# c turned by VectorE in 32x32 blocks and the convolution evicted by ScalarE, in a two-layer kernel on one core

## What is computed

```python
# layer 0: a channel mixing drawn from cond, then a feed-forward with a top-1 of 4 low-rank experts
agg_w = einsum('bk,koi->boi', softmax(mlp(cond)), weight)
y     = einsum('boi,bih->boh', agg_w, x) + agg_b[:, :, None]
x     = x + y @ W_up.T + one_hot(argmax(y @ gate.T + ebias)) . (y @ A) @ B
# layer 1: a grouped convolution along the positions (9 taps, 4 groups of 8 channels), then top-2 of 8 experts
c     = conv1d(x, wconv, pad=4, groups=4) + (cond @ c_weight.T)[:, :, None] + fside[None, :, None]
x     = x + c @ W_base.T + b_base + sum over the two best experts of p_e * (c @ A_e) @ B_e
```

## Time and profile before

| what | value |
|---|---|
| median of 3 runs | 400.89 us (400.55 to 401.44) |
| the profiled execution's own time | 400.67 us |
| its span in the trace | 398.9 us |
| granted TensorE clock, mean | 0.996 |
| PE, weight loads, DVE, ACT, POOL busy | 96%, 89%, 68%, 26%, 40% |
| DMA | 77 GB/s, queue 1 26.1% of 16 engines |

### The profile page before, as it was taken

The page is one execution under the profiler, slowest core; times in us unless marked ns, Lnnn a source line. Parts: engine busy times, 40 slices in busy tenths (PEclk is TensorE's granted clock), DMA queues, the critical chain, the costliest instruction groups (busy, mean ns, idle before and its releaser), DMA issues.

```text
span 398.9 us, 8234 instructions
## 1 busy us (share of the span) xinstructions
PE 383.5 (96%) x2615; PEld 354.9 (89%) x2615; DVE 270.0 (68%) x837; ACT 103.5 (26%) x251; POOL 160.4 (40%) x146
## 2 busy tenths in 40 slices
PE   4999999999999999999999999999999999999995
PEld 2887999989999999999999999999999999999984
DVE  4568667657766676777667767676677676766553
ACT  4733222222122222221222222212222222222211
POOL 4314444243444443334444433344444333444420
PEclk9989999999999999999999999999999999999999
DMA  5803342212122222112222321222222212222111
GB/s 131 268 15 114 116 140 81 80 32 65 64 78 79 79 79 74 37 61 65 79 79 79 79 78 30 63 66 79 79 79 79 58 50 64 66 79 79 54 53 55
DMA packets 31404, 30.75 MB, mean 77 GB/s; under 512 B 4740, under 2 KB 21556, under 8 KB 31392
## 3 DMA queue, kind: packets, MB, share of 16 engines
q1 hardware_dynamic: 31184, 30.19, 26.1%
q0 software_dynamic: 208, 0.41, 0.4%
HBM read 13.79 MB, written 8.40 MB: 56 GB/s over the span
## 4 chain that ended last, share of the span: by engine, by line
PE 86%; issue 2%; DVE 1%; DMA 1%; ACT 1%; SPq 0%; DVEq 0%
PE ps_base L912 18%; PE ps_conv L865 17%; PE ps_up L829 15%; PE ps_base L917 9%; PE ps_up L834 7%; PE ps_mix L789 7%; PE ps_base L883 5%; PE ps_ct L894 4%; PE ps_up L776 2%; PE ps_turn L768 2%; DMA xq<-x1p 1%; PE ps_turn L760 1%; SPq L293 0%; DVE x1p L598 0%; DVE c L680 0%
## 5 line engine op out<-in xcount | busy, mean ns | idle before, releaser
L364 POOL TENSOR_TENSOR y_lo<-y,y_hi 128x512 fp32r<-128x512 f32 x31 | 40.1, 1293 | 198.8 <-ACT y_hi L407 198.8
L912 PE MATMUL ps_base<-base_hi,c_hi 128*128 128x392 f32 (+1 forms) x256 | 77.7, 320 | 1.1 <-ACT c_hi L458 1.1
L912 PE MATMUL ps_base<-base_lo,c_hi 128*128 128x392 f32 (+1 forms) x256 | 75.0, 310 | 0.0
L829 PE MATMUL ps_up<-up_hi,y_hi 128*128 128x292 f32 (+1 forms) x256 | 67.9, 292 | 0.7 <-ACT y_hi L407 0.7
L829 PE MATMUL ps_up<-up_lo,y_hi 128*128 128x292 f32 (+1 forms) x256 | 67.5, 291 | 0.0
L508 DVE TENSOR_TENSOR mix_w<-gsum,quad 128x64 f32<-128x64 f32 x64 | 48.1, 753 | 6.6 <-DVE gl L648 5.3
L371 POOL TENSOR_TENSOR x1b<-x1p,bbase_s 128x512 f32<-128x512 f32 x32 | 50.1, 1566 | 4.1 <-DVE ot L688 4.1
L912 PEld LDWEIGHTS ps_base<-base_hi,c_hi 128*128 128x128 f32 x256 | 48.4, 189 | 1.5 <-DVE ot L688 1.5
L829 PEld LDWEIGHTS ps_up<-up_hi,y_hi 128*128 128x128 f32 x256 | 48.9, 191 | 0.9 <-ACT y_hi L407 0.9
L829 PEld LDWEIGHTS ps_up<-up_lo,y_hi 128*128 128x128 f32 x256 | 48.9, 191 | 0.0
L917 PE MATMUL ps_base<-base_hi,c_lo 128*128 128x392 f32 (+1 forms) x256 | 48.4, 311 | 0.0
(11 more groups left out here) (156 smaller groups left out, 626.7 us busy)
## 6 DMA issues: line engine op xcount, KB each, us to landing
xt<-in_x SPq DMA_DIRECT2D x32, 256.0 KB, 3.0
xq<-x1p SPq DMA_DIRECT2D x128, 64.0 KB, 2.2
out_x<-ot SPq DMA_DIRECT2D x32, 256.0 KB, 3.0
rows<-agg_rows SPq DMA_DIRECT2D x2, 597.0 KB, 4.1
wup_raw<-in_L_ffn_W_up SPq DMA_DIRECT2D x2, 512.0 KB, 5.5
wbase_raw<-in_L_ffn_W_base SPq DMA_DIRECT2D x2, 512.0 KB, 5.2
rows<-agg_rows SPq DMA_DIRECT2D x1, 598.0 KB, 4.7
rows<-agg_rows SPq DMA_DIRECT2D x1, 256.0 KB, 4.0
```

Of the source, the lines that this page charges most:

```text
L364: pool.tensor_tensor(y_lo[:], y32[:], y_hi[:], ALU.subtract).then_inc(ylo_done, 1)
L829: pe.matmul(into, y_hi[:, k], w[:, k, cols], start=(k == 0 and w is up_hi), stop=False, skip_group_check=True)
L912: pe.matmul(ps_base[:, j, 0:width], c_hi[:, q], w[:, q, j, 0:width], start=(q == 0 and w is base_hi), stop=False, skip_group_check=True)
```

## The change

- `c32` is written by ACT, `conv_out`: four activations (Identity, with `biasT` as bias from SBUF), one a batch, each 128x128 from `ps_conv`.
- `c32` is turned by DVE, `turn_c`: two transposes of 128x256, which turn each 32x32 block by itself and write `ps_ct`. The four transposes of PE are gone, and its other stages keep their order.
- `ps_ct` then holds on partitions (q, m modulo 32) and in columns (batch, m divided by 32, o): the chunks of the base product are blocks of 128 neighbouring positions and no longer remainders. So POOL reorders `wbase_raw`, `a1_raw` and `g1_raw` in the setup (`base_p` in four copies of 128x512, two of them ahead of the first `y_lo`; `a1_p`; `g1_p`), and the fill of the layer 1 gate moves from the place before the first step to the end of the fills.
- `ot` is summed in two halves of 128x256 (`out_sum`), and each bank of `ps_base` is freed by its own half.

```diff
+            pool.wait_ge(in_base[0], 16)
+            for dc in range(KC // 2):
+                pool.tensor_copy(by_chunk(base_p[:, dc]), chunk_rows(wbase_raw[:, dc])).then_inc(basep_ready, 1)
             pool.wait_ge(y32_done, 1)
             pool.wait_ge(yhi_done, 1)
             pool.tensor_tensor(y_lo[:], y32[:], y_hi[:], ALU.subtract).then_inc(ylo_done, 1)
+            pool.wait_ge(in_base[1], 16)
+            for dc in range(KC // 2, KC):
+                pool.tensor_copy(by_chunk(base_p[:, dc]), chunk_rows(wbase_raw[:, dc])).then_inc(basep_ready, 1)
+            pool.wait_ge(in_a1, 16)
+            pool.tensor_copy(by_chunk(a1_p[:]), chunk_rows(a1_raw[:])).then_inc(a1p_ready, 1)
+            pool.wait_ge(in_gate, 16)
+            pool.tensor_copy(by_chunk(g1_p[:]), chunk_rows(g1_raw[:])).then_inc(g1p_ready, 1)
...
+            def conv_out(t):
+                act.wait_ge(conv_done, t + 1)
+                after(act, ct_done, t * 2)
+                for b in range(SPT):
+                    act.activation(c32[:, b], ps_conv[:, 0, b * NM:(b + 1) * NM], ACT.Identity,
+                                   bias=biasT[:, bass.ds(t * SPT + b, 1)]).then_inc(c32_done, 1)
...
+            def turn_c(t):
+                after(dve, clo_done, t)
+                for half in range(2):
+                    dve.wait_ge(c32_done, t * SPT + (half + 1) * (SPT // 2))
+                    dve.transpose(ps_ct[:, 0, half * HALF:(half + 1) * HALF],
+                                  c32[:, half * (SPT // 2):(half + 1) * (SPT // 2)].rearrange("p b m -> p (b m)"))\
+                        .then_inc(ct_done, 1)
...
                 if once(i - 1):
-                    dve.wait_ge(conv_done, i)
-                    after(dve, ct_done, i - 1)
-                    for half in range(2):
-                        b2 = slice(half * SPT // 2, (half + 1) * SPT // 2)
-                        dve.tensor_tensor(c32[:, b2], ps_conv[:, 0].rearrange("p (b m) -> p b m", b=SPT)[:, b2],
-                                          biasT[:, bass.ds((i - 1) * SPT + half * (SPT // 2), SPT // 2)].unsqueeze(2)
-                                          .to_broadcast([P, SPT // 2, NM]), ALU.add).then_inc(c32_done, 1)
+                    turn_c(i - 1)
                 if once(i - 2):
-                    dve.tensor_tensor(ot[:, par].rearrange("p (j d) -> p j d", j=2), ps_base[:, :, 0:HALF],
-                                      x1b[:, par].rearrange("p (j d) -> p j d", j=2), ALU.add)\
-                        .then_inc(out_done, 1)
+                    out_sum(i, par, 0)
+                    out_sum(i, par, 1)
...
-                if once(i - 1):
-                    after(pe, clo_done, i - 1)
-                    for b in range(SPT):
-                        if b % (SPT // 2) == 0:
-                            pe.wait_ge(c32_done, (i - 1) * 2 + 1 + b // (SPT // 2))
-                        mm = pe.transpose(ps_ct[:, 0, b * P:(b + 1) * P], c32[:, b], ident[:])
-                    mm.then_inc(ct_done, 1)
                 if once(i + 1):
                     mix(i + 1, 1 - par)
```

More of the change, by code:

```diff
@@ L181, in adaln_ffn @@
                                         for q in range(NQ)], NQ, NM, None, None))
[L182 to L188, removed]
+        for k in range(KC):
+            cols = slice(k * P, (k + 1) * P)
+            fills.append(((basep_ready, KC), [base_p[:, dc, cols] for dc in range(KC)], KC, P,
+                          base_hi[:, k, :, 0:HALF].rearrange("m j (k d) -> m j k d", k=2),
+                          base_lo[:, k, :, 0:HALF].rearrange("m j (k d) -> m j k d", k=2)))
+        fills.append(((a1p_ready, 1), [a1_p[:, k * P:(k + 1) * P] for k in range(KC)], KC, P,
                       base_hi[:, :, 0, HALF:HALF + P], base_lo[:, :, 0, HALF:HALF + P]))
@@ L251, in load_base @@
                 sp.dma_start(wbase_raw[:, k2], w_base.rearrange("(k p) h -> p k h", p=P)[:, k2])\
-                    .then_inc(in_base, 16)
+                    .then_inc(in_base[half], 16)
             sp.dma_start(cond_s[:], cond).then_inc(in_cond, 16)
@@ L369, in body @@
                     pool.wait_ge(x1_done, i + 1)
-                    after(pool, out_done, i - 1)
+                    after(pool, out_done, (i - 1) * 2)
                     pool.tensor_tensor(x1b[:, par].rearrange("p (m q) -> p m q", q=NQ),
@@ L403, in high_part, with z_high @@
                     act.activation(fills[n][4], fill_bank(n), ACT.Copy).then_inc(fill_hi, 1)
+            def z_high(t):
+                act.wait_ge(zt_done, t + 1)
+                act.activation(zT[:], ps_turn[0:3 * Z0, 0, 0:P], ACT.Copy).then_inc(zhi_done, 1)
+            def conv_out(t):
[4 more added lines that the diff above has]
+                                   bias=biasT[:, bass.ds(t * SPT + b, 1)]).then_inc(c32_done, 1)
             def y_high(t):
@@ L446, in body @@
                 if once(i):
-                    act.wait_ge(zt_done, i + 1)
-                    act.activation(zT[:], ps_turn[0:3 * Z0, 0, 0:P], ACT.Copy).then_inc(zhi_done, 1)
+                    z_high(i)
+                if once(i - 1):
+                    conv_out(i - 1)
                 if isinstance(i, int) and i == 0:
@@ L453, in body @@
                 if once(i - 1):
-                    act.wait_ge(ct_done, i)
+                    act.wait_ge(ct_done, i * 2)
                     for half in range(2):
@@ L575, in _ @@
             y_sum(0)
-            for n in range(3, NF0):
+            for n in range(3, NF1):
                 low_part(n)
@@ L607, in z_low, with out_sum @@
                     .then_inc(zT_ready, 1)
+            def turn_c(t):
[5 more added lines that the diff above has]
+                        .then_inc(ct_done, 1)
+            def out_sum(i, par, j):
+                if j == 0:
+                    dve.wait_ge(delta_done, i - 1)
+                    dve.wait_ge(x1b_done, i - 1)
+                    after(dve, stored[par], pair_count(i, par, -4))
+                dve.tensor_tensor(ot[:, par, j * HALF:(j + 1) * HALF], ps_base[:, j, 0:HALF],
+                                  x1b[:, par, j * HALF:(j + 1) * HALF], ALU.add).then_inc(out_done, 1)
             G1 = 5
@@ L811, in _ @@
             pe.wait_ge(taps_ready, 1 + NQ)
+            pe.wait_ge(y32_done, 1)
             for s in range(SLOTS):
@@ L839, in body @@
                         fill(n)
[L840 removed]
+                    pe.wait_ge(fill_lo, NF1)
                 if isinstance(i, int) and i == 1:
@@ L851, in body @@
                     pe.wait_ge(xqhi_done, i)
-                    after(pe, c32_done, (i - 1) * 2)
+                    after(pe, c32_done, (i - 1) * SPT)
                     for part, (rhs, weights) in enumerate(((xq_hi, (conv_hi, conv_lo)), (xq_lo, (conv_hi,)))):
@@ L902, in body @@
                 if once(i - 1):
-                    after(pe, out_done, i - 1)
                     for j, width, done in ((0, L1W, basegate_done), (1, HALF, base_done)):
+                        after(pe, out_done, (i - 2) * 2 + 1 + j)
                         for q in range(NQ):
```

32 lines of the change are left out of this document (16 added, 16 removed).

## The result

With the change the kernel takes **427.5 us** (median of 4 runs, 426.3 to 428.8); the kernel before took 401.0 beside it (4 runs). The ratio is 1.069, 95% interval 1.065 to 1.073: slower, as forecast, and 2.7 us above the 424.8 of the forecast. The profiled execution took 426.26 us, its span is 424.4 us.

What follows compares the result with a forecast made beforehand. The bound was taken to be a loop from T (a convolution's end) through DVE, POOL, `mix_w` and `turn_z`. 400.67 + 29 x 0.81 (23.5) + 0.4 = 424.6, as median 424.8 us; range 406 to 438.

Steps and rivals of the forecast that it cites:

- The bound: Loop from T (a convolution's end) through DVE, POOL, `mix_w`, `turn_z` to the next T: delay between T and `y32` lengthens the step.
- PE's transposes are worth nothing: On PE, the transposes' 0.46 us a step leave, but `c_lo` comes no sooner from DVE; nothing credited.
- Start of the second transpose: On DVE, after ACT's last `c32` piece: T + 1.23 where the second addition started at T + 0.49, +0.74 us a step.
- Transposes of 0.42, 0.34 apart: On DVE, each 128x256 transpose taken to last 0.42 us and start 0.34 apart, like the additions that go.
- `ot` in halves, +0.07: On DVE, `ot` as two halves takes 2 x 0.34 us for 0.61, +0.07 a step.
- The sum, +0.81 a step: In the loop, +0.74 for the second transpose's start and +0.07 for `ot`, over 29 steps 23.5 us; 0.4 for the ends.
- PE's idle, 1.2 us a step in front of the base product: PE waits at the base product's `c_hi` and `c_lo` parts: 0.74 plus the 0.46 us its transposes gave back.
- PE's own path, 10.98 and 11.72: PE's step without its `turn_z` wait of 0.43 us: 10.98 us before, 11.72 with the change, under the loop's 12.36.
- slips past POOL: Rival: the first `mix_w` starts before POOL's `xq_lo` and escapes the hold; +0.23 us a step, 408 us; chance 0.18.
- ACT's pieces or the transposes are slow: Rival: ACT's `c32` pieces do not overlap, 437 us, or with slow DVE transposes 447; chance 0.08 beyond 438.
- PE is the bound, faster: Rival: PE never waits for `c_lo`, so 32 x 0.46 = 14.7 us go, 386 us; chance 0.05.

Runs made afterwards that it cites:

- seven kernels on one line: The kernel before, it with one DVE addition more, the changed kernel and four variants, all with `mix_w` held: step is `y32`'s end plus 7.59 to 7.64 us.
- the mask in PSUM: `mix_w`'s second input, the mask `quad`, read from PSUM from tile 2 on: 417.1 us in the changed kernel, 395.5 us in the kernel before.
- the kernel without any hold: The changed kernel with `mix_w`'s mask `quad` read from PSUM: 417.1 us, ratio 1.041 to the kernel before, 11.99 us a step.

## Why the prediction was right

**The bound.** *Right.* The loop from T over DVE's operations, `y_hi`, POOL's block, `mix_w` and `turn_z` is what sets the time of both kernels: seven kernels on one line, and the mask in PSUM takes its wait away in both.

**PE's transposes are worth nothing.** *Right*, and for one more reason than was given. The forecast had the loop hide them. Without the loop they are still worth nothing, since they filled a wait for c.

**Start of the second transpose.** *Too small.* T + 1.23 was taken, it is 1.35. ACT's pieces last 0.369 as the one row of such a piece said, but they start 0.25 apart and not 0.22, and the first 0.18 after T and not 0.15. The lower bound of 0.17 apart rests on 0.86 ns a column, which no row of the forecast gives (0.38 less 0.28 over 128 columns is 0.8); as copies the pieces did start 0.16 apart. The Trainium skill's budget (ScalarE: Activation LUTs, Rules for kernel authors) gives an estimate of 0.41 for a piece; run one after the other they would have put the start at 1.84. The trace has 0.369 and an overlap, so the time that page gives, 442, is too long. Its advice, to leave additions to VectorE, is borne out by the kernel in which DVE adds: 11 us less.

**Transposes of 0.42, 0.34 apart.** *Right in size*: 0.433 long and 0.36 apart where nothing holds them. *Missed*: behind a transpose that waits for ACT, `ot` starts 0.49 later. In the kernel before, `ot` followed the second addition by 0.40 in the mean; the forecast had read that from one longer step, 0.48.

**`ot` in halves, +0.07.** *Right*: 0.07, shown by putting it back.

**The sum, +0.81 a step.** By its terms `y32`'s end moved by 0.86 (start of the second) + 0.09 (to `ot`) + 0.07 (`ot`) - 0.02 = 1.00, and the rest of the loop was 0.05 shorter: **+0.94** in the mean of 23 steps. Of this 0.05, the one slipped step makes 0.01, and in the others 0.04 lies in front of `xq_lo`, which starts 0.20 after `xq_hi` ends in the kernel before and 0.16 with the change; no run shows why. The steps came out at 12.30 and 12.43 where 12.1 and 12.4 were forecast. Over the whole execution the 31 intervals grew by 26.5 us (21.7 in these 23, 4.8 in the eight at the ends) and the end behind the last T by 0.7, where the forecast had 23.5 and 0.4. The first T came 1.7 sooner (35.4 for 37.1), which I do not credit to the change: with the same setup and the mask in PSUM it is at 36.8, and over all traces here it lies anywhere from 34.8 to 37.3. That makes 25.5 for 23.9. The 1.7 is luck: without it the forecast would have been 4.3 us under and not 2.7. The other 1.0 of the 2.7 us is the place of the profiled execution among the runs, 1.2 under the median now and 0.2 before.

**PE's idle, 1.2 us a step in front of the base product.** *Right in place, split otherwise*: 0.76 in front of the base product and 0.47 in front of `c_lo`, 1.23. `c_hi` was there at 2.23 and not at 2.08.

**PE's own path, 10.98 and 11.72.** *Wrong*, and the step whose reasoning failed. Taking away a wait of 0.43 does not leave a step 0.43 shorter: 0.2 of PE's work lay in the shade of the wait. It is 11.23, and 11.99 with the change. It did not matter for the forecast, as both stand below the loop (11.41 and 12.355), but the rival "slips past POOL" was priced at 408 by it, with steps of 11.64, where the one step that slipped took 12.05 and the kernel without any hold has 11.99 and 417 us.

**The rivals.** *`mix_w` slips past POOL* happened in one of the 23 steps, the one shown above, and in none of the 23 of the other seven kernels that keep both inputs in SBUF. The forecast had "none of the looped steps slips now", but in the kernel before, the first two steps of the loop do. The margin between the two starts shrank as forecast, from 0.34 in the mean to 0.14 in the held steps (0.10 to 0.18). With one addition more in the kernel before it was 0.01 to 0.05 in every other step, and that held too. So the steps stayed on the right side by little, and the runs do not show what keeps them there. *ACT's pieces or the transposes are slow*: a part of it, 0.25 apart, is in the result. *PE is the bound, faster*: PE was busiest in both and gained nothing. The rule of the Trainium skill (Perfetto Trace Analysis, Identifying the Most-Contended Engine) would have sent one to PE, whose weight loads were the busiest too, with 89%. The 96% of the profile's page were true, and the 4% that were missing decided.

## What to carry to other kernels

The engine that is 96% busy may still wait once in every step, and it is that wait's chain that a change has to shorten; follow it back by first operands until it closes, and count what the change puts into it. Before crediting an engine with work taken off it, ask what it would have done at that time: here it would have waited for the very data it was turning. And a wait that is taken away gives back less than its length where it hid work behind it.

## What the runs showed of the hardware

- A transpose of 128x256 fp32 by DVE, from SBUF to PSUM in 32x32 blocks, takes 433 ns and follows the one before by 0.36, like an addition of that size; 128x512 takes 0.73. Where each was released by another engine, it was 459 ns, and the next of DVE's instructions started 0.49 after the second.
- An activation of 128x128 from PSUM takes 369 ns with a bias from SBUF and 282 ns as a copy. In a train the starts are 0.25 and 0.16 apart.
- A DVE instruction of 128x64 with both inputs in SBUF took 0.58 to 1.31 us where a POOL instruction was already running (changed kernel), and 0.23 where it started first. The same with one input in PSUM took 0.22.
- A DVE transpose that waits by semaphore for the instruction just ahead started 0.11 after that one's end. One that waits for the instruction before that started 0.1 before the end of the one just ahead.
